# A third buffer of row numbers and weights for the second layer's experts, and the next gather placed behind the issue of the second scatter

## The reference, cut to what matters

```
scores = softmax(flat_x @ gate_w.T).T                # (16, 2048)
topk_weight, topk_idx = top_k(scores, C)             # C = 256 per expert
xg = flat_x[topk_idx]                                # gather
g = einsum('ecd,eid->eci', xg, Wg)
u = einsum('ecd,eid->eci', xg, Wu)
h = gelu(g) * u                                      # 1024 wide
eo = einsum('eci,edi->ecd', h, Wd) * topk_weight[..., None]
flat_out = zeros.at[topk_idx].add(eo)                # scatter with addition
```

## Time and profile before

| what | value |
|---|---|
| timed runs | 2988.44 us median of 3 (2987.21 to 2988.63) |
| profiled execution, span from first to last instruction | 2968.3 us |
| what lies around the span (median of the timed runs less the span) | 20.1 us |
| PE busy over the span | 2648.8 us (89%) |
| PE busy, last stage, 14 experts from 2600.00 to 2933.67 us | 314.15 us of 333.67 us |
| granted clock, mean of the span | 0.945 of full speed |

### The profile page before, as it was taken

One profiled execution on the slowest core, in us unless ns is written; L12 is line 12 of the kernel. 1 busy time (PEld: TensorE's weight loads), 2 busy tenths in 40 slices (PEclk: granted clock), 3 DMA queues, 4 the chain that ended last, 5 costly groups with the idle time before them and its releaser, 6 DMA issues. The chain is left out here.

```text
span 2968.3 us, 40239 instructions
## 1 busy us (share of the span) xinstructions
PE 2648.8 (89%) x16440; PEld 1563.7 (53%) x16441; DVE 1453.5 (49%) x2235; ACT 1084.1 (37%) x1885; POOL 681.2 (23%) x364
## 2 busy tenths in 40 slices
PE   7679999999999999999959969989889998699997
PEld 4256534754275425653248844453543633477876
DVE  5566347832875357733711144446444553644432
ACT  4664245622563245523413222433434333011111
POOL 0255034900763045701520020000000000022222
PEclk9879999999999999999979977999999998799999
DMA  5540002100030003000059920010100102044452
GB/s 195 204 179 23 0 1 111 44 1 0 1 141 14 1 1 121 34 0 1 8 207 341 333 55 8 1 37 8 22 22 1 23 8 92 15 149 149 160 167 78
DMA packets 62127, 219.26 MB, mean 74 GB/s; under 512 B 12293, under 2 KB 28122, under 8 KB 45178
## 3 DMA queue, kind: packets, MB, share of 16 engines
q1 hardware_dynamic: 45802, 187.39, 17.5%
q0 software_dynamic: 9568, 18.75, 2.6%
q10 hardware_dynamic: 6576, 10.57, 1.0%
HBM read 172.50 MB, written 39.99 MB: 72 GB/s over the span
## 5 line engine op out<-in xcount | busy, mean ns | idle before, releaser
L642 PE MATMUL psum<-arena 128*128 128x256 f32 (+7 forms) x4224 | 1096.6, 411 | 65.0 <-ACT arena L1506 11.5
L642 PEld LDWEIGHTS psum<-arena 128*128 128x128 f32 (+1 forms) x4224 | 680.3, 197 | 430.7 <-issue 317.2
L2468 POOL TENSOR_TENSOR arena<-arena 128x1024 f32<-128x1024 f32 x128 | 299.6, 2381 | 98.3 <-DVE arena L1969 83.5
L1969 DVE TENSOR_TENSOR_SCAN arena<-arena,psum 128x512 f32<-128x512 f32 x256 | 290.9, 1201 | 22.4 <-PE psum L783 14.5
L783 PEld LDWEIGHTS psum<-arena 128*128 128x128 f32 x2048 | 236.7, 193 | 49.2 <-ACT arena L1536 40.3
L783 PE MATMUL psum<-arena 128*128 128x128 f32 x2048 | 249.0, 279 | 2.0 <-issue 1.9
L2503 POOL DMA_INDIRECT arena<-xn,arena x32 | 31.6, 987 | 902.8 <-DVE arena L2410 851.5
L2475 POOL TENSOR_TENSOR arena<-arena 128x1024 f32<-128x1024 f32 x32 | 75.9, 2373 | 652.4 <-ACT arena L1624 652.4
L2063 DVE SCALAR_TENSOR_TENSOR arena<-psum,arena 128x1024 f32<-128x1024 f32 x128 | 156.9, 1244 | 80.5 <-PE psum L928 80.1
L1624 ACT ACTIVATE arena<-arena 128x1024 f32<-128x1024 f32 x128 | 146.7, 1146 | 110.1 <-DVE arena L2063 109.9
L1230 PE MATMUL psum<-arena 32*128 32x512 f32 x512 | 175.1, 675 | 3.1 <-DVE arena L2261 3.1
(11 more groups left out here) (292 smaller groups left out, 3007.9 us busy)
## 6 DMA issues: line engine op xcount, KB each, us to landing
arena<-in_W SPq DMA_DIRECT2D x46, 1024.0 KB
arena<-c_rows SPq DMA_DIRECT2D x32, 512.0 KB, 3.9
arena<-in_Wg SPq DMA_DIRECT2D x16, 1024.0 KB, 4.9
arena<-in_Wu SPq DMA_DIRECT2D x16, 1024.0 KB, 7.7
arena<-in_Wd SPq DMA_DIRECT2D x16, 1024.0 KB, 10.1
arena<-in_xT SPq DMA_DIRECT2D x8, 512.0 KB, 5.9
zs_all<-arena SPq DMA_DIRECT2D x4, 1024.0 KB, 3.9
ut_all<-arena SPq DMA_DIRECT2D x4, 1024.0 KB, 8.7
```

What stands on the lines that cost most here:

```text
L642: r = mm(dst, w, x, start=i == 0, stop=i == len(pairs) - 1)
L1969: V.tensor_tensor_scan(hs[n % 3][:, c, :], dA[n % 2][:, c, :], bank[4 + c], 0.0, ALU.mult, ALU.add)\
L2468: nc.gpsimd.tensor_tensor(h, h, c_all[:, n % CBUFS, :].unsqueeze(1).broadcast_to([P, 2, L]), ALU.mult)\
```

## The change

There are three buffers of `idx` and `w_slot` in place of two, so `take_picks(e)` waits for the scatters of e - 3 and not of e - 2. On GpSimd the wait for the second scatter's landing goes from behind that scatter to just ahead of the next scatter, which is one expert later; the wait for the first half's landing stays ahead of the second half. The gather of expert n + 2 is written behind the scatters of n, where it came first in the following turn. Expert 1's gather comes ahead of the wait for the stored shared part.

```
-        idx, w_slot = [take(2).bitcast(u32) for _ in range(2)], [take(2) for _ in range(2)]
+        idx, w_slot = [take(2).bitcast(u32) for _ in range(3)], [take(2) for _ in range(3)]
...
-                j = e % 2
+                j = e % 3
...
-                if e >= 2:
-                    dve.wait_ge(added.sem, added.at(32, e - 2))
+                if e >= 3:
+                    dve.wait_ge(added.sem, added.at(32, e - 3))
...
-                    V.tensor_scalar(eo[j][:, hf, :], bank[6 + hf][:, 0:D], w_slot[j][:, hf:hf + 1],
+                    V.tensor_scalar(eo[j][:, hf, :], bank[6 + hf][:, 0:D], w_slot[n % 3][:, hf:hf + 1],
...
-                    pool.indirect_dma_start(xg1[e % 2][:, hf, :], None, xn1, on(ap=idx[e % 2][:, hf:hf + 1], axis=0))\
+                    pool.indirect_dma_start(xg1[e % 2][:, hf, :], None, xn1, on(ap=idx[e % 3][:, hf:hf + 1], axis=0))\
                         .then_inc(got_x[e % 2].sem, 16)
 
             gather(0)
+            gather(1)
             pool.wait_ge(st_o.sem, st_o.at(0, B))
             for n in range(E1):
-                if n + 1 < E1:
-                    gather(n + 1)
                 for hf in range(2):
                     if hf == 0 and n + 1 == E1:
                         pool.wait_ge(we_free.sem, we_free.at(1, n))
                     else:
                         pool.wait_ge(eo_ready.sem, eo_ready.at(1, n))
-                    pool.indirect_dma_start(out, on(ap=idx[n % 2][:, hf:hf + 1], axis=0), eo[n % 2][:, hf, :], None,
+                    if hf == 1:
+                        pool.wait_ge(added.sem, added.at(16, n))
+                    elif n >= 1:
+                        pool.wait_ge(added.sem, added.at(32, n - 1))
+                    pool.indirect_dma_start(out, on(ap=idx[n % 3][:, hf:hf + 1], axis=0), eo[n % 2][:, hf, :], None,
                                             compute_op=ALU.add).then_inc(added.sem, 16)
-                    pool.wait_ge(added.sem, added.at(16 * (hf + 1), n))
+                if n + 2 < E1:
+                    gather(n + 2)
```

## The result

| what | before | after |
|---|---|---|
| timed runs | 2987.82 us median of 4 (2979.24 to 2988.63) | 2953.14 us median of 4 (2952.3 to 2954.98) |
| ratio, 95% interval | | 0.9903 (0.9884 to 0.9923) |
| span of the profiled execution | 2968.3 us | 2951.5 us |
| 14 turns of TensorE in the last stage | 333.67 us | 310.85 us |
| last transposes to the end of the span | 38.6 us | 36.2 us |

The ratio is a gain of 29 us (23 to 35) on 2988, clear of noise though small beside the whole. The changed kernel was timed again in two later sets, at 0.9909 (0.9889 to 0.9929) and 0.9912 (0.9882 to 0.9941). So the mechanism has to be looked at apart from the size and from the base that it was taken off.

A forecast was written before the change was run, and what follows sets the result against it. PE waits in each of 14 turns for the next expert's gather, held up by the second scatter's landing. 24.4 us less 0.6 (gather beside scatter) and 0.8 (clock) leaves 23.0 off 2988.44: 2965.4 us, range 2962.8 to 2973.5.

The forecast's parts named there:

- A turn without the wait, 22.09 us: Last stage: PE's turn length read off expert 0, whose gather has no scatter ahead; 14 such turns are 309.3 us.
- Start and landing of the gather: GpSimd's gather starts 0.30 us behind the second scatter's issue or after row numbers, lands in 2.8 us; 0.6 us taken off.
- rivals 1 (gather behind the scatter's data): Gather moves only once the second scatter has landed: 13.8 us gain, 2974.6 us; 16% with what lies between.
- 2 (stretched gather): Gather slowed as the first scatter is, landing 4.7 us later per turn: 3054 us; 2% with smaller such losses.
- 4 (no effect): The gather waits for something else, so the change does nothing; 3% together with rival 3.
- X unchanged: X, the second scatter's start counted from the turn's start, stays at 10.3 to 12.1 us.
- The cover of 0.55 us: In the usual turn the gather's second half lands 0.55 us ahead of the transposes' need at 17.97 us.
- The clock, 0.8 us: Half of the 1.7 us from PE's one clock fall, taken off the gain as falls in timed runs were unknown.
- Rival 3: No change because PE's clock falls in every turn, 23.8 us in all: about 2988 us; 3% together with rival 4.
- The end, nothing: Work behind 2933 us, after the turns, was forecast to stay as it was.
- 24.4 us: What PE gives up at most in the profiled execution: 14 turns at 333.67 us against 309.3 us.
- The 20.1 us around the span: Difference between the timed 2988.44 us and the profiled span of 2968.3 us, claimed to stay.

The follow-up runs named there:

- e3: Changed kernel, but GpSimd still waits for the second scatter's landing ahead of the gather; ratio to before 0.9949 (0.9931 to 0.9966).
- e4: Changed kernel, but the row numbers on VectorE again wait for the scatters of two experts before; ratio to before 0.9994 (0.9978 to 1.0010).
- e6: Changed kernel with the gather placed between the two scatters; ratio to before 0.9883 (0.9858 to 0.9909).
- e1: Kernel before, run again without any edit; ratio to before 1.0002 (0.9985 to 1.0019).
- e8: Kernel before, run a third time without any edit; 14 turns in 338.5 us.
- e9: Kernel before, without GpSimd's wait for the landing of the very last scatter; ratio to before 0.9981 (0.9962 to 1.0000).
- e5: Kernel before, with two more matmuls per turn ahead of PE's wait for the gather; ratio to before 1.0012 (0.9996 to 1.0028).
- e10: Changed kernel with GpSimd's wait for the very last landing put back at its end; ratio to before 0.9895 (0.9859 to 0.9932).
- e2: Changed kernel, run again without any edit; ratio to before 0.9909 (0.9889 to 0.9929).
- e12: Changed kernel, run a third time without any edit; ratio to before 0.9912 (0.9882 to 0.9941).

## Why the forecast was right in its mechanism and wrong in its size

**The chain.** Right. Row numbers waited for the second landing, the gather for the row numbers, PE for the gather. e3 and e4 show that both waits had to go.

**A turn without the wait, 22.09 us.** Right: 22.09 to 22.11 us in every turn of e6, 309.4 us in all against 309.3.

**Start and landing of the gather.** Right: 0.30 us behind the issue of the second scatter. Landing beside a scatter: 2.8 us in the median, 3.8 at most,

```profile
DMA to landing us min/median/max: 2.7/2.8/3.8
```

against 2.6/2.8/2.9. The 0.6 us that I took off became 0.8, 0.4 and 0.4 us of wait in the three traces, and turns that are 0.8 to 1.5 us longer in all than those of e6. So rivals 1 (gather behind the scatter's data), 2 (stretched gather) and 4 (no effect) are out. VectorE adds nothing to GpSimd's issue either: 1.01 and 0.97 us as before, with a product of VectorE (2690.75 to 2691.17 us) inside the first of them.

**X unchanged.** Wrong by half a us, at a small price. It was 10.3 to 12.1 and is 10.8 to 12.8 us; the first four turns have the largest. The first scatter doesn't take longer to land. The landings of the scatters in the changed profile answer to the 3.7/3.9/10.4 of the earlier trace rows:

```profile
DMA to landing us min/median/max: 3.7/3.9/10.3
```

What moved is the second scatter. In the fourth turn of the kernel before it starts 0.27 us behind the first one's landing (issued at 2674.54, landed 10.36 us later, the second issued at 2685.17), and so it does in most turns. In the changed kernel it starts 0.79 us behind the landing in most turns and 1.10 in the fourth (2676.84, 10.27 us, 2688.21). e3 and e4 tell these apart: e3, whose wait for the landing stands right behind the first scatter, has the 0.27 us, and e4, whose wait stands behind the one on `eo_ready`, has the 0.79. So it is the new place of the wait on GpSimd, which the forecast put at nothing. The cover of 0.55 us took it up in all but the first, third and fourth turn, and e6, where the gather doesn't stand behind it, shows that this is worth 0.8 to 1.5 us.

**The clock, 0.8 us.** The first term that was mis-sized. I took half of the one fall seen, so the term could only make the gain smaller; it did not allow for more falls than one. Its 1.7 less 0.8 leaves 0.9 us of gain from the clock. The three other traces of the kernel as it was before (e1, e8 and, in its turns, e9) have three falls each; with the first that is a mean of 2.5, 4.3 us. Their waits are longer too (20.9, 21.0 and 23.7 us against 19.5), 1.8 us in the mean of the four. So the turns take 337.8 us in that mean, and the gain in the turns is 337.8 - 310.5 = 27.3 us, not the 22.8 between the first two traces. The trace that I read, with 2968.3 and 1.8 us, is the shortest execution of this kernel seen. Rival 3 had the right mechanism with the wrong sign: with the waits the falls go. What falls are worth in the timed runs is less sure than in the traces, since e5 removed them and was no faster.

**The end, nothing.** The second term: 2.4 us, missed altogether. I followed GpSimd's wait into the next expert and did not ask where the last one goes. The code showed it: the wait at L2518 stands behind the last scatter too, and the changed loop has none there. e9 and e10 show that this wait is what the 2.4 us are.

**The sum.** 27.3 and 2.4 are 29.7 us; the means of all executions, 2985.6 and 2956.4, differ by 29.2. The forecast's 23.0 is 6.7 us too low, 4.3 in the turns (more falls and longer waits than in the trace read) and 2.4 at the end. The step that failed is that 24.4 us, read off one execution, was taken as what PE gives up "at most", and so as the far edge of the range.

**The base and the range.** "The 20.1 us around the span" is no such thing: it is 1.8 us, and the other 18 us are the distance of one short execution, with its clock at 0.945, from the median. That did not move the forecast, which was taken off the timed median; but it was the sign that executions of this kernel differ by far more than the 0.7 us that three timed runs showed and that I put into the range. They differ by 27 us from lowest to highest. The base, 2988.4, lies 2.8 us above the mean of 77 executions. On the other side 2953.14 is the median of four runs within 3 us of each other and lies 3.3 us below the mean of 16. So of the 12.3 us between forecast and time about half is a gain that was forecast too small, and the other half is which executions happened to be timed. Chance is not all of it: the mean of the 16, 2956.4, is below the range too, by 6.4 us. The bound of 0.2% for what can be told from no change was too narrow in the same way.

## What to carry to other kernels

When a profiled span and the timed median differ by more than a few us, don't call the difference overhead: compare a run's own time with its own span, and take the spread of executions into the range. Price a wait of TensorE that repeats every turn with what the clock does behind it, since here 18 us of added wait cost 31, and let that term go both ways when only one trace was read. When a wait is moved into the next turn, ask what it did behind the last one, and when one event is waited for in two places, take both away.

## What the runs showed of the hardware that was not expected

- In the last stage of the traces 32 waits of PE ahead of the transposes were 2.0 to 4.0 us long. Behind 24 of them the granted clock was at half, at 1.7 us each; behind 8 it stayed at 1.00, as behind the 2.67 us of the forecast's trace and the 2.43 us of e9. So the length alone doesn't decide. Behind waits up to 1.8 us (e3, e5) it never fell, nor in the turns of the changed kernel.
- The unchanged work ahead of the last stage took from 2574.1 to 2597.9 us in 14 traces; the two ends had mean clocks of 0.945 and 0.937 over their spans, and 2288.7 and 2305.9 us of PE's busy time for the same instructions.
- A scatter whose wait for the landing ahead of it stands behind another wait started 0.79 us behind that landing, and 0.27 us where the landing was waited for first (after and e4 against before and e3).
- A second waiter on the last landing lengthened the end of the program by 2.4 us: 38.6 to 38.7 us in the six traces with it and no fall there (before, e1, e8, e3, e5, e10), 36.2 to 36.3 in the six without (after, e2, e12, e4, e9, e6).
